# Opening of an attention and expert kernel: zeroed products on TensorE, another order of loads, key weight after the query fold, constants ahead of the branch

## The reference

```python
# layer 1: attention from x to a context, latent keys and queries
h = layernorm(x)                               # 8 x 256 x 256
kv_c = ctx @ W_kvc                             # latent width 64
q_c  = h @ W_dq                                # latent width 96
q_nope, q_rope = q_c @ W_uq, rope(q_c @ W_qr)  # 16 heads, 128 and 64 wide
k_nope, k_rope = kv_c @ W_uk, rope(kv_c @ W_kr)
scores = (q_nope @ k_nope.T + q_rope @ k_rope.T) * scale
good = (k_ids <= seg) & (k_ids >= seg - 8)     # seg = itok, a key index for each row
x = x + softmax(where(good, scores, -1e30)) @ (kv_c @ W_uv) @ W_o
# layer 2: each row goes to its 2 best of 8 experts
h = layernorm(x)
best2 = top_k(h @ gate_w + gate_b, 2)
x = x + mean over best2 of relu(h @ expert_w[e] + expert_b[e])
```

## Time and profile before

| | us |
|---|---|
| median of three runs | 395.16 |
| lowest and highest | 394.85, 395.56 |
| span of the profiled execution, first to last instruction | 391.2 |
| TensorE busy in the span | 354.0 (90%) |
| DVE, ACT, POOL busy | 288.3, 264.0, 234.1 |

### The profile page before, as it was taken

How to read it: one execution, slowest core, us unless ns; L and a number is a source line. 1 busy time by engine, 2 the same in 40 slices (tenths; PEclk the granted TensorE clock), 3 DMA queues, 4 the chain that set the end, 5 groups by cost and what they waited for, 6 DMA issues and landing times.

```text
span 391.2 us, 10358 instructions
## 1 busy us (share of the span) xinstructions
PE 354.0 (90%) x2507; PEld 289.2 (74%) x2507; DVE 288.3 (74%) x1395; ACT 264.0 (67%) x907; POOL 234.1 (60%) x326
## 2 busy tenths in 40 slices
PE   1989999998999999999999999999998788999940
PEld 0856877786688878888878888788886577888730
DVE  2367887788888889888788888888889566444455
ACT  1347777788878878778888788788787544445430
POOL 4616555468976777677677676776764355455500
PEclk9999999999999999999999999999999999999985
DMA  8964040000000000000000000000000354543178
GB/s 277 349 215 188 7 105 3 1 3 29 0 30 1 30 20 7 27 0 27 14 14 27 0 27 0 27 27 0 30 2 28 95 161 131 148 132 121 34 239 316
DMA packets 15093, 28.27 MB, mean 72 GB/s; under 512 B 2892, under 2 KB 10719, under 8 KB 14416
## 3 DMA queue, kind: packets, MB, share of 16 engines
q1 hardware_dynamic: 11408, 20.25, 16.1%
q0 software_dynamic: 2960, 6.94, 5.0%
q10 hardware_dynamic: 688, 0.64, 0.6%
HBM read 17.81 MB, written 10.91 MB: 73 GB/s over the span
## 4 chain that ended last, share of the span: by engine, by line
PE 65%; DVE 12%; issue 10%; POOL 7%; DMA 2%; ACT 2%; DVEq 0%; SPq 0%; POOLq 0%; ACTq 0%
PE psum L1133 11%; PE psum L672 8%; PE psum L673 8%; PE psum L674 8%; PE psum L1090 7%; PE psum L1203 6%; PE psum L1117 5%; POOL prob L1361 2%; DVE x_all L1554 2%; POOL q_sb L1347 2%; PE psum L1180 2%; DVE nsc L1622 2%; DMA wcat<-in_w_kvc 2%; PE psum L369 2%; PE psum L1012 1%
## 5 line engine op out<-in xcount | busy, mean ns | idle before, releaser
L1228 ACT ACTIVATE prob<-nsc,nmax 128x128 f32<-128x128 f32 x256 | 100.8, 396 | 36.3 <-DVE nmax L1622 35.5
L1347 POOL TENSOR_TENSOR q_sb<-rope_a,rope_b 128x256 f32<-128x256 f32 x64 | 47.5, 742 | 59.2 <-DVE rope_b L1585 55.1
L1361 POOL TENSOR_TENSOR prob<-prob,prec 128x512 f32<-128x512 f32 x64 | 67.2, 1050 | 7.4 <-DVE prec L1593 7.4
L1133 PE MATMUL psum<-kT_all,qT 128*128 (+1 forms) x512 | 68.6, 277 | 1.1 <-ACT qT L1271 1.1
L1622 DVE CUSTOM_DVE_ANT_0 nsc<-psum,mask 128x128 f32<-128x128 f32 x256 | 58.6, 284 | 13.0 <-PE psum L1133 13.0
L1133 PEld LDWEIGHTS psum<-kT_all,qT 128*128 128x128 f32 x512 | 62.1, 192 | 2.7 <-ACT qT L1271 2.4
L1415 POOL DMA_INDIRECT halves<-jout,jidx x33 | 32.2, 976 | 30.3 <-DVE jidx L1526 13.7
L1228 ACT ACTIVATION_READ_ACCUMULATOR prob<-nsc,nmax 128x1 f32 x256 | 48.4, 189 | 0.0
L1090 PE MATMUL psum<-ident,q_sb 128*128 128x128 f32 x256 | 41.9, 286 | 2.2 <-POOL q_sb L1347 1.8
L1090 PEld LDWEIGHTS psum<-ident,q_sb 128*128 128x128 f32 x256 | 26.8, 140 | 21.7 <-POOL q_sb L1347 13.6
L1203 PE MATMUL psum<-pT,v_cur 128*64 128x256 f32 x256 | 41.8, 405 | 0.0
(11 more groups left out here) (204 smaller groups left out, 878.1 us busy)
## 6 DMA issues: line engine op xcount, KB each, us to landing
wanted<-slots SPq DMA_DIRECT2D x33, 129.0 KB, 2.4
wo_raw<-in_w_o SPq DMA_DIRECT2D x2, 1024.0 KB, 14.9
we_raw<-in_expert_w SPq DMA_DIRECT2D x1, 2048.0 KB, 7.8
half<-halves SPq DMA_DIRECT2D x4, 512.0 KB, 7.1
x_all<-in_x SPq DMA_DIRECT2D x2, 640.0 KB, 17.4
slots<-pad_row SPq DMA_DIRECT2D x8, 129.0 KB, 3.4
we_raw<-in_ctx_near SPq DMA_DIRECT2D x1, 1024.0 KB, 11.2
out<-x_all SPq DMA_DIRECT2D x2, 512.0 KB, 4.6
```

The costliest lines, as they stand in the source:

```text
L1133: mm = pe.matmul(B_S[r][:, h, :], qT[r][:, h, :], batch_keys, start=True, stop=True)
L1228: e = act.activation(prob[r][:, h, :], nsc[r][:, h, :], ACT.Exp, bias=nmax[r][:, h:h + 1], scale=-1.0, accum_out=psum_h[r][:, h:h + 1])
L1347: pool.tensor_tensor(q_sb[1 - r][:, :, KVC:P], rope_a[1 - r][:], rope_b[1 - r][:], ALU.add).then_inc(m["rope_joined"], 1)
L1361: pool.tensor_tensor(p[:], p[:], prec[1 - r][:, :].unsqueeze(2).to_broadcast([P, HG, P]), ALU.mult).then_inc(m["prob_normed"], 1)
```

## The change

Five edits, all ahead of the branch or moved there:

1. DVE clears a bf16 tile `warm` (128 x 512), and TensorE multiplies it with itself 17 times into bank 4, whose contents nobody reads, before it waits for anything else. The tile takes its room from `late_room`, a space filler.
2. ACT issues wdq and wqr first, then wkvcT, wkr and wkvc. SP issues the context ahead of the query rope table.
3. On TensorE the first half of the fold goes ahead of the flag's product, and `wkk` from the front to the end of the opening. On DVE the flag's comparison goes ahead of the copy of `wkk`.
4. POOL builds the constants in the opening, behind its four loads and ahead of its waits for the branch.
5. `general_pe`, the other side of the branch, gets a wait on wkk_sb.

```diff
+        warm = tmp("warm", [P, 4 * P], BF16)
+        tmp("late_room", [P, 14 * P])
...
             sp.dma_start(wukT[:], w_uk_t).then_inc(S("ld_wuq"), 16)
+            sp.dma_start(ctxT, ctx_near.rearrange("p c (b k) -> p c b k", b=B)).then_inc(S("ld_ctx"), 16)
             sp.dma_start(ropeq[:], rope[0:L, :].rearrange("(t p) (a n) -> p t a n", p=P, a=2)).then_inc(S("ld_ropeq"), 16)
-            sp.dma_start(ctxT, ctx_near.rearrange("p c (b k) -> p c b k", b=B)).then_inc(S("ld_ctx"), 16)
...
         def opening_act(act):
+            act.dma_start(wdq[:], w_dq).then_inc(S("ld_wdq"), 16)
+            act.dma_start(wqr[:], w_qr.rearrange("c (h r) -> c h r", r=R)).then_inc(S("ld_wqr"), 16)
             act.dma_start(wkvcT[:], w_kvc_t).then_inc(S("ld_kv"), 16)
             act.dma_start(wkr[:], w_kr).then_inc(S("ld_kv"), 16)
             act.dma_start(wkvc, w_kvc).then_inc(S("ld_kv"), 16)
-            act.dma_start(wdq[:], w_dq).then_inc(S("ld_wdq"), 16)
-            act.dma_start(wqr[:], w_qr.rearrange("c (h r) -> c h r", r=R)).then_inc(S("ld_wqr"), 16)
...
             pool.dma_start(eb[:], expert_b.rearrange("e (a n) -> (e a) n", n=P)).then_inc(S("ld_eb_wg"), 16)
+            constants(pool)
             pool.wait_ge(S("kidx_done"), 1)
...
         def opening_dve(dve):
+            dve.memset(warm[:], 0.0).then_inc(S("warm_set"), 1)
             batch_stats(dve, 0)
...
+            dve.wait_ge(S("ok_mm"), 1)
+            dve.tensor_scalar(flag[:], B_E[0:1, 0:1], float(P), None, ALU.is_ge).then_inc(S("flag_done"), 1)
             dve.wait_ge(S("wkk_mm"), 1)
             dve.tensor_copy(wcat[:, :, KVC:P], B_X[:, 0:DC * R].rearrange("p (c n) -> p c n", c=DC)).then_inc(S("wkk_sb"), 1)
-            dve.wait_ge(S("ok_mm"), 1)
-            dve.tensor_scalar(flag[:], B_E[0:1, 0:1], float(P), None, ALU.is_ge).then_inc(S("flag_done"), 1)

         def opening_pe(pe):
+            pe.wait_ge(S("warm_set"), 1)
+            for _ in range(17):
+                pe.matmul(bank[4][:, :], warm[:, 0:P], warm[:], start=True, stop=True)
+
             pe.wait_ge(S("ident_done"), 1)
-            pe.wait_ge(S("ld_kv"), 48)
-            for c in range(DC):
-                mm = pe.matmul(B_X[:, R * c:R * c + R], wkvcT[:, P * c:P * c + P], wkr[:], start=True, stop=True)
-            mm.then_inc(S("wkk_mm"), 1)
-
             pe.wait_ge(m["x_normed"], TPB)
...
+            pe.wait_ge(S("ld_wuq"), 32)
+            fold_q(0)
             pe.wait_ge(S("row_ok_done"), 1)
             pe.wait_ge(S("ones_set"), 3)
             pe.matmul(B_E[0:1, 0:1], row_ok[:], ones_col[:], start=True, stop=True).then_inc(S("ok_mm"), 1)
-            pe.wait_ge(S("ld_wuq"), 32)
-            fold_q(0)
...
             fold_q(1)
+            pe.wait_ge(S("ld_kv"), 48)
+            for c in range(DC):
+                mm = pe.matmul(B_X[:, R * c:R * c + R], wkvcT[:, P * c:P * c + P], wkr[:], start=True, stop=True)
+            mm.then_inc(S("wkk_mm"), 1)
...
         def general_pe(pe):
+            pe.wait_ge(S("wkk_sb"), 1)
...
         def general_pool(pool):
-            constants(pool)
...
-                if isinstance(i, int) and i == -2:
-                    constants(pool)
```

More of the change, by code:

```diff
@@ L142, in tmp @@
             return prep_only.enter_context(nc.sbuf_tensor(name, shape, dt))
-        tmp("late_room", [P, 16 * P])
+        warm = tmp("warm", [P, 4 * P], BF16)
+        tmp("late_room", [P, 14 * P])
         wkvcT = tmp("wkvcT", [KVC, D])
```

## The result

| | before | after |
|---|---|---|
| median of five runs | 395.56 us | 401.65 us |
| lowest and highest | 394.85, 396.60 | 400.69, 401.95 |
| ratio to before, 95% interval | | 1.015 [1.0131, 1.0168] |
| span of the profiled execution | 391.2 | 399.4 |

The change costs 6.1 us (1.5%), where I had forecast a gain of 1.05. The profiled execution of after took 401.24 us, 1.8 more than its span, and every later run of any version was 1.7 to 1.9 us above its span.

The account below looks back on a forecast made before the run. TensorE, busy for most of the span, paces the walk, so an earlier opening moves everything: `wkk` ends at 14.4, plus 1.1 and 3.0 gives 18.5 against 19.57, 1.05 us off 395.16, so 394.1 us, range 393.3 to 396.6.

Parts of the forecast that it names:

- (a): Load the first half of the fold waits for: by byte count lands at 9.1 us, a microsecond later than now.
- (b): Last load of ld_kv on ACT's queue: lands at 13.5 us, just hidden behind the second fold's end at 13.8.
- (c): TensorE's opening: clock rises under the zeroed products and stays up, folds 1.8 us each, latents 1.0, `wkk` ends at 14.4.
- fourth rival: Clock doesn't rise, or falls again, before the folds: `wkk` ends at 17.2, marker 21.3, time 396.9 us; chance 0.24.
- (e): POOL's constants, 4.58 us of work, move into 4.57 us of its idle time in the opening and cost nothing.
- marker: Start of `key_rows(0)` on DVE: from 19.57 to 18.5 us, and the end of the kernel earlier by as much.
- (d): DVE behind the end of `wkk`: copy and branch 1.1 us, then 3.0 us of queued work up to the marker.
- (f): Base of the forecast: the median lies 4.0 us above the profiled span of 391.2.

Follow-up runs that it names:

- e1: The change with its fourth part undone: POOL builds the constants in the walk, as before; 397.45 us, ratio 1.0086 to before.
- e11: The whole change with 28 zeroed products at the front instead of 17, and 7 and 5 more in the walk; 396.20 us, ratio 1.0013 to before.
- e5: The change, but POOL waits for the two normalized tiles of batch 0 before it builds the constants; 399.38 us, ratio 1.0106 to before.
- e7: e1 with the copy of `wkk` moved from DVE's opening to ACT in the walk; 396.09 us, ratio 0.9998 to before.
- e4: The change without zeroed products and early constants, so the new load and work order alone; 399.74 us, ratio 1.0107 to before.
- e2: The kernel before with the early constants (fourth part) alone; 394.97 us, ratio 0.9991 to before.
- e12: e1 with zeroed products added at the front and in the walk as in e9, copy of `wkk` on DVE; 396.79 us, ratio 1.0033 to before.
- e3: The kernel before with the clear of `warm` and the 17 zeroed products alone; 394.70 us, ratio 0.998 to before.
- e6: e1 with the loads issued in the old order; 397.82 us, ratio 1.0063 to before.
- e8: The kernel before with the 17 zeroed products in the opening and 7 and 5 more in the walk; 393.51 us, ratio 0.9943 to before.
- e9: e7 with 8 more zeroed products between transposes and first fold, and 7 and 5 in the walk; 395.62 us, ratio 0.9979 to before.

## Why the prediction was wrong

**(a) The fold's load, forecast 9.1.** wukT, issued at 1.72, landed 8.1 us later, at 9.8 (DMA issues of after):

```profile
wukT<-in_w_uk_t SPq DMA_DIRECT2D x1, 512.0 KB, 8.1
```

My count of bytes took a load as done when all that was issued ahead of it had moved. In the first 10 us SP's queue moved 2.04 MB, of which x, wuqT and wukT are 1.57; 0.47 MB were of the context and others, issued behind and moved ahead. The direction was right, and 0.7 us too small. By the Trainium skill (DMA: Bandwidth & Descriptors, section Issuing engines are not separate DMA queues) DMAs of several issuing engines run on the same 16 engines and interleave; here loads of one issuer did so as well.

**(b) ld_kv, forecast 13.5.** wcat, issued at 2.95, landed 10.3 us later, at 13.2, and PE asked for it only at 17.9. Right, and not what decided.

**(c) The clock, forecast to rise and stay.** This is the step that failed. It rose at 7.1, but PE then had 0.96 us of work in 7.2 to 10.5, and the clock was low again from 10.6. Fold 0 took 2.71 and not 1.8, the latents 1.81 and not 1.0, fold 1 2.27. `wkk`'s end, T, came to 18.5 instead of 14.4. My fourth rival described this, with 17.2 for T and 396.9 for the time; what it lacked is (e), which put the fold's start at 11.0 (the late load alone put it at 10.0 in e1), and all that came behind the marker. The experiment on it is e11: with 12 more products in the walk, where the clock fell a second time, the cost of the whole change goes from 1.5% to 0.1% [-0.2, 0.5], although the opening stays as slow as it was.

The fall isn't certain: e5 and e7 have the same pause of PE (transposes until 8.5, fold from 10.45), and e7's clock fell at 10.4 while e5's stayed; it had risen at 7.0 in e7 and at 5.8 in e5. By the Trainium skill (TensorE: Matmul & The Clock Gate, section Part 4: PE-mode transpose) a transpose doesn't count as busy the same way as a product. The two executions show that either outcome is possible behind nearly the same rows, so they neither bear it out nor refute it.

**(d) The chain behind `wkk`, forecast copy + branch 1.1, then DVE's 3.0.** Measured 19.58 - 18.55 = 1.03 and 22.45 - 19.58 = 2.87. Right. e4 shows that this chain, which I priced and accepted, is what the new order costs up to the marker (2.11); it was to be paid for by the faster folds.

**(e) The constants, forecast at nothing.** The term failed. I asked only what waits for POOL and found idle time of 4.57 us; I didn't ask whom POOL's work disturbs. The first of the two L344 took 3380 ns in place of 411:

```profile
L344 DVE TENSOR_SCALAR xn<-x_all,mv_all,rstd_all x2: 395/1888/3380, 6.5 to 9.8; 128x256 f32<-128x256 f32 x2
```

e2 and e5 show that the constants beside it do this (3.91 with them, 0.73 without), and the clear is the only long one of them, filling 1.8 us of that time. It is hidden in the old order and open in the new one: e2 costs nothing that can be measured, part 4 on top of e1 0.6%. What the stall itself costs in time stays open: e5 removes it and its ratio isn't clearly below that of after, and e11 has it and isn't slower than e12. By the Trainium skill (SBUF — State Buffer, section Who interferes with whom) DVE and GpSimd have a pair of ports in common, which is held for a whole instruction while the other is blocked; a DVE operation that uses both its ports (a one-source copy or tensor_scalar from SBUF to SBUF in a two-port mode), or one with two SBUF sources beside a GpSimd read, can be caught. Both rows agree in that DVE was held: 3.38 us at the clear, and 1.27 beside POOL L315. The length doesn't follow from it: the norm's record starts 1.1 us before that of the clear and outlasts it by 0.4; POOL's recorded times are rough. The rule was there to be read before I costed part 4 at nothing.

**(f) The base, forecast span + 4.0.** The true distance is 1.8; the 4.0 contained 2.2 us by which the profiled execution was faster than the median. The gap of 4.0 was in the table and should have warned me that this kernel's executions differ by more than my whole gain. Why the profiled one was fast stays open; a higher mean clock isn't the reason, since executions of before with 0.987, above its 0.984, took 394.5 to 395.8.

**What came behind the marker.** I took a marker d us earlier to be an end d us earlier. That failed as well, and it weighs more than the opening. e5 is nearly the opening that I forecast: the clock stayed up, T and marker came 0.7 and 0.5 us late (the marker at 19.02), and its four runs are 1.1% slower than before all the same. Between marker and 32 us the shift grew by what the clock did there: by 2.0 to 2.3 us in after, e1, e3, e4 and e6, where it was low for 6.8 us; by 1.3 to 1.4 in e2, e5 and e7, where it was low for 3.4; by 0.0 to 0.4 in e8 to e12, where 12 products fill the stretch and it stayed up. The profiled before kept its clock there without them. The meeting of DVE and POOL, the late load and the late falls are decided further behind.

The sum by ratios: the new order by itself +4.2 us (e4), with the zeroed products +3.4 (e1; the intervals of the two overlap), with the constants +5.9. How much of each is path and how much clock, one trace of each doesn't separate. But the time at the lower level, (1 - clock) x 2 x span with the median of the mean clocks, is 27 us in after, 22 in e1, 24 in e5, 15 to 16 in before, 14.5 in e9 and 11 in e8, each with the 10 to 13 us behind the last product.

**Open.** Why the clock falls at 326 to 331 us in some executions (after, e5, e9) and not in others is not settled: the work is the same and no run filled that stretch. Before the falls at 309 and 310 us (e9, e12) stands the wait for a late load, whose cause isn't known. Nor was it tried to move POOL L315 away from DVE's operation at 102 us; that it is a chance meeting is argued from two traces that have it (after, e5) and those that don't.

## What to carry to other kernels

When idle time of an engine is to be filled, look at both sides: who waits for the engine, and which operation of its neighbour runs there now. A stall that costs nothing in one order of the work can be open in another, which takes away the work that hid it, so price edits in the order in which the kernel will have them. An early start is worth what is left of it further on: follow it past the marker in more than one execution. Warming TensorE paid here when the thin stretches behind were filled as well: 17 products gave 1.85 us at the marker and 0.2% of the time, within its uncertainty (e3), and the same with 12 more in two thin places gave 0.6% (e8). Before relying on one profiled execution, compare its span with the spread of the times.

## What the runs showed of the hardware

- The granted clock behind the same instructions differs from execution to execution (e5 and e7 at 10.4 us), and what a fall to 1.2 GHz cost behind the marker went with its length: 1.3 to 1.4 us for 3.4 us at the lower level (e2, e5, e7 near 25 us; after, e5, e9 near 330), 2.0 to 2.3 for 6.8 us (after, e1, e3, e4, e6). In e1 the two groups of times, 396.3 and 401.5, differ in their mean clock.
- Beside a POOL clear of 128 x 2048 f32, 1.82 us by its record, a DVE operation of 0.41 us took 3.38, and in e5 one of 0.18 us took 1.40.
- In e12 a DVE cast of 96 x 128, 0.22 us in most other traces, took 1.19 beside the same clear:

```profile
15.47 1.80 POOL L542 MEMSET bias<- 128x2048 f32 x1
...
16.16 1.19 DVE L1664 CAST qc_hi<-qc_all 96x128 fp32r<-96x128 f32 x1 [0.74 <-issue]
```
